# A two-layer recurrent and attention net on one core: sums, gating and output projection between the layers rearranged over GpSimd, TensorE, VectorE and ScalarE

## The reference, cut to what matters

```
xn = layernorm(x)
# layer 0: a gated pair of recurrences, and 8 experts (top 2, capacity 640 rows each)
for t in range(256):                       # for each of the 16 sequences
    h_ssm = silu(h_ssm @ A.T + bx[t]);  y_ssm = h_ssm @ Cw.T + Cb + dx[t]
    h_rnn = GRU(h_rnn, ih[t]);          y_rnn = h_rnn @ proj_w.T + proj_b
    s[t]  = g0[t] * y_ssm + g1[t] * y_rnn
moe = w0 * expert[top0](xn) + w1 * expert[top1](xn)     # silu(moe) below
x   = x + s * silu(moe)
# layer 1: attention with 16 heads of 64, and 160 experts (top 8)
xn = layernorm(x)
x  = x + attention(xn) * silu(ffn160(xn))
```

## Time and profile before

| what | value |
|---|---|
| time before, median of 3 runs | 2086.22 us (2082.82 to 2088.34) |
| time of the profiled execution | 2083.28 us |
| its span in the profile | 2081.5 us |
| its mean granted TensorE clock | 0.938 |
| busy: PE, DVE, ACT, POOL | 1823.4, 1272.7, 888.1, 625.7 us |

### The profile page before, as it was taken

The page is one execution under the profiler, slowest core; times in us unless marked ns, Lnnn a source line. Parts: engine busy times, 40 slices in busy tenths (PEclk is TensorE's granted clock), DMA queues, the critical chain, the costliest instruction groups (busy, mean ns, idle before and its releaser), DMA issues.

```text
span 2081.5 us, 49942 instructions
## 1 busy us (share of the span) xinstructions
PE 1823.4 (88%) x14389; PEld 1623.3 (78%) x14390; DVE 1272.7 (61%) x4624; ACT 888.1 (43%) x2899; POOL 625.7 (30%) x661
## 2 busy tenths in 40 slices
PE   4699999999999999369999999688888988888786
PEld 2467999999997777239999998677777788787785
DVE  4444444544554434888888888344444677777776
ACT  2212444444442211316666665344444555555453
POOL 0074000000006400016677773000000555555551
PEclk9799999999999975669999999899999999999997
DMA  9511011111001100301111112444444211111111
GB/s 377 238 47 37 23 36 35 36 44 40 25 26 47 30 0 0 159 9 48 48 49 52 51 50 101 147 141 149 149 145 141 58 40 39 38 40 40 38 40 54
DMA packets 153497, 149.29 MB, mean 72 GB/s; under 512 B 16931, under 2 KB 134374, under 8 KB 153062
## 3 DMA queue, kind: packets, MB, share of 16 engines
q1 hardware_dynamic: 130820, 100.98, 14.6%
q0 software_dynamic: 21760, 46.18, 7.5%
q10 hardware_dynamic: 866, 1.51, 0.2%
HBM read 70.95 MB, written 77.66 MB: 71 GB/s over the span
## 4 chain that ended last, share of the span: by engine, by line
PE 67%; DMA 11%; DVE 10%; issue 8%; ACT 2%; POOL 1%; DVEq 1%; ACTq 0%; POOLq 0%; SPq 0%
DMA rows_g<-ys_dram,slot 10%; PE ps_y L735 8%; PE ps_t L940 5%; PE ps_up L1042 5%; PE ps_y L793 4%; PE ps_up L784 4%; PE ps_t L1053 4%; PE ps_up L916 4%; PE ps_y L929 3%; PE ps_t L753 3%; PE ps_t L751 3%; PE ps_rec L750 3%; PE ps_rec L748 3%; PE ps_rec L884 2%; PE ps_rec L1020 2%
## 5 line engine op out<-in xcount | busy, mean ns | idle before, releaser
L479 POOL DMA_INDIRECT rows_g<-ys_dram,slot x256 | 242.7, 948 | 529.8 <-DMA ys_dram<-slots_y 346.7
L623 ACT ACTIVATE probs<-ps_up,negmax 128x256 f32<-128x256 f32 x512 | 240.5, 483 | 323.9 <-DVE negmax L1447 323.9
L469 POOL DMA_INDIRECT xs_dram<-xn_tok,slot x256 | 249.4, 974 | 314.6 <-DVE slot L1349 215.1
L940 PE MATMUL ps_t<-v_sb,probsT 128*128 128x64 f32 x2048 | 261.2, 271 | 2.1 <-DVE ctx_sb L1430 1.5
L940 PEld LDWEIGHTS ps_t<-v_sb,probsT 128*128 128x128 f32 x2048 | 252.7, 194 | 4.3 <-issue 4.2
L735 PE MATMUL ps_y<-zeros 128*128 128x512 bf16 x752 | 219.8, 382 | 0.0
L1206 DVE SCALAR_TENSOR_TENSOR mixn<-ps_rec,cols_sb,th_r 128x16 f32<-128x16 f32 x256 | 59.8, 234 | 245.1 <-PE ps_rec L750 143.1
L1447 DVE TENSOR_REDUCE negmax<-ps_up 128x2 f32<-128x512 f32 x256 | 164.7, 685 | 31.2 <-PE ps_up L916 30.9
L916 PE MATMUL ps_up<-kT,qT 64*128 64x256 f32 x1536 | 127.7, 299 | 60.6 <-DVE kT L1403 60.0
L916 PEld LDWEIGHTS ps_up<-kT,qT 64*128 64x128 f32 x1536 | 101.7, 190 | 81.2 <-issue 60.8
L929 PE MATMUL ps_y<-misc,probs 128*128 128x128 f32 x1024 | 163.7, 283 | 0.6 <-ACT probs L623 0.5
(11 more groups left out here) (241 smaller groups left out, 4386.0 us busy)
## 6 DMA issues: line engine op xcount, KB each, us to landing
xs_dram<-zeros SPq DMA_DIRECT2D x52, 512.0 KB, 9.3
slots_x<-xs_dram SPq DMA_DIRECT2D x88, 256.0 KB, 3.0
ys_dram<-slots_y SPq DMA_DIRECT2D x84, 256.0 KB, 2.5
slots_x<-xs_dram SPq DMA_DIRECT2D x41, 128.0 KB, 2.1
ys_dram<-slots_y SPq DMA_DIRECT2D x40, 128.0 KB, 1.8
gate<-w_gate SPq DMA_DIRECT2D x1, 5120.0 KB, 20.7
down<-w_down SPq DMA_DIRECT2D x1, 5120.0 KB, 15.2
w_sb<-w POOLq DMA_DIRECT2D x16, 256.0 KB, 4.8
```

What stands on the lines that cost most here:

```text
L469: nc.gpsimd.indirect_dma_start(xs_dram, bass.IndirectOffsetOnAxis(ap=slot[:, n, k:k + 1], axis=0), xn_tok[:, n, :], None).then_inc(scatter ...
L479: nc.gpsimd.indirect_dma_start(rows_g[:, i % 16, :], None, ys_dram, bass.IndirectOffsetOnAxis(ap=slot[:, i // TOPK1, i % TOPK1:i % TOPK1 + ...
L623: nc.scalar.activation(probs[:, a, i, :], ps_s[a][:, T * i:T * i + T], ACT.Exp, bias=negmax[:, a, i:i + 1], accum_out=sums[:, j % 4, i, a: ...
L940: last = nc.tensor.matmul(ps_ctx[:, P * i + HD * a:P * i + HD * a + HD], probsT[:, a, kc, P * i:P * i + P], v_sb[:, j % 2, kc, HD * a:HD * ...
```

## The change

Five edits, all between the layers or for them:

1. `hist_s`'s bias row is written by GpSimd at the start of the kernel (64 partitions in place of 32), and the recurrent step writes only the 64 partitions of the state. The memset after the recurrence is gone.
2. The sum of the expert rows goes to GpSimd: per tile two products with a weight per token and one sum, 128 columns each, issued one tile behind the two gathers (`sum_rows`).
3. The output projection runs in groups of four tiles, each kind of result in one bank of 512 columns. TensorE waits once in four tiles, ScalarE takes the tanh of a quarter behind each of the first four groups, and VectorE makes silu behind each even group.
4. The product with s and the sum with x go to GpSimd, in pieces of 512 columns (`sil_ready`, `gated`, `x1_ready`). Mean and subtraction of layer norm 2 begin behind the odd groups from the fourth; the squares go to another buffer. The casts of the weights come before the product with the reciprocal, and ScalarE's scaling of the query weights, and an empty sigmoid, before the copies of the turned tokens. The weight loads wait for `var_ready` too.
5. In the placement loop, the offset comes in by one more matmul of one row (line 919 of the changed kernel), and VectorE's add is gone: it multiplies by the mask straight from PSUM, which is also `place_read`.

```diff
@@ GpSimd
+            nc.gpsimd.memset(hist_s[64:128, :, :], 2.0).then_inc(bias_rows, 1)
+            def sum_rows(n):
+                nc.gpsimd.tensor_scalar(xn_tok[:, n, :], xn_tok[:, n, :], w0[:, n, 0:1], None, ALU.mult) \
+                    .then_inc(row_scaled, 1)
+                nc.gpsimd.tensor_scalar(second[:, n, :], second[:, n, :], w0[:, n, 1:2], None, ALU.mult) \
+                    .then_inc(row_scaled, 1)
+                pool.wait_ge(row_scaled, 2 * n + 2)
+                nc.gpsimd.tensor_tensor(xn_tok[:, n, :], xn_tok[:, n, :], second[:, n, :], ALU.add) \
+                    .then_inc(acc_final, 1)
...
+                if n:
+                    sum_rows(n - 1)
...
+            for g in range(NG):
+                tok = slice(512 * g, 512 * g + 512)
+                pool.wait_ge(sil_ready, g // 2 + 1)
+                pool.wait_ge(y_used, g + 1)
+                nc.gpsimd.tensor_tensor(sil[:, tok], sil[:, tok], s_all[:, tok], ALU.mult).then_inc(gated, 1)
+                pool.wait_ge(gated, g + 1)
+                nc.gpsimd.tensor_tensor(x_all[:, tok], x_all[:, tok], sil[:, tok], ALU.add).then_inc(x1_ready, 1)
@@ SyncE
             sp.wait_ge(x1_ready, NG)
+            sp.wait_ge(var_ready, 2)
@@ ScalarE
-            for n in range(NT):
-                act.wait_ge(y_ready, n + 1)
-                nc.scalar.mul(gin[:, 1, n // 2, 128 * (n % 2):128 * (n % 2) + 128], ps_up[n % 2][:, 0:128],
-                              gate[:, n, 0:1]).then_inc(y_scaled, 1)
+            for g in range(NG):
+                act.wait_ge(y_ready, g + 1)
...
+                if g < 4:
+                    act.wait_ge(acc_final, 8 * g + 8)
...
+                if g == 5:
+                    square(1, squares, 0)
+            for c in range(1, 4):
+                square(1, squares, c)
+            deviation(1)
+            act.wait_ge(attn_loaded, 16 * 10)
@@ TensorE, output projection
-            pe.wait_ge(bias_rows, 1)
-            for n in range(NT):
-                b, h = n // 2, n % 2
-                if n >= 2:
-                    pe.wait_ge(y_scaled, n - 1)
-                    pe.wait_ge(y_used, n - 1)
...
+            for g in range(NG):
+                if g >= 2:
+                    pe.wait_ge(y_scaled, 4 * (g - 1))
+                    pe.wait_ge(y_used, g - 1)
+                for n in range(4 * g, 4 * g + 4):
...
+                last.then_inc(y_ready, 1)
@@ TensorE, placement
+            pe.wait_ge(offs_ready, 1)
             pe.wait_ge(probs1_ready, NT)
...
+                nc.tensor.matmul(dst, ones[0:1, :], offs[0:1, :], start=True, stop=False)
                 if n:
                     nc.tensor.matmul(dst, upper_b[0:NT, n - 1:n].to_broadcast([NT, P]), tile_tot,
-                                     start=True, stop=False)
-                nc.tensor.matmul(dst, upper_b, chosen[:, n, :], start=(n == 0), stop=True).then_inc(place_mm, 1)
+                                     start=False, stop=False)
+                nc.tensor.matmul(dst, upper_b, chosen[:, n, :], start=False, stop=True).then_inc(place_mm, 1)
@@ VectorE
-            V.memset(hist_s[64:96, :, :], 2.0).then_inc(bias_rows, 1)
...
+                if g % 2 == 0:
+                    q = slice(512 * g, 512 * g + 1024)
+                    dve.wait_ge(silu_th, g // 2 + 1)
...
+                elif g >= 3:
+                    dve.wait_ge(sil_ready, g // 2)
+                    dve.wait_ge(x1_ready, g - 1)
+                    centre(1, g // 2 - 1)
...
+            centre(1, 3)
+            variance(1, squares)
...
+            scale_rows(1)
...
             for n in range(NT):
                 dve.wait_ge(place_mm, n + 1)
-                V.tensor_tensor(place[:, n, :], ps_rec[n % 2][:, 0:E1], offs, ALU.add).then_inc(place_read, 1)
+                V.tensor_tensor(place[:, n, :], ps_rec[n % 2][:, 0:E1], chosen[:, n, :], ALU.mult) \
+                    .then_inc(place_read, 1)
                 if n >= 1:
-                    placed(n - 1)
-                if n >= 2:
-                    places_of(n - 2)
+                    places_of(n - 1)
```

More of the change, by code:

```diff
@@ L121, in build @@
         newn = sb("newn", [P, 16])
+        sil = gin[:, 0, :, :].rearrange("p b t -> p (b t)")
+        s_all = gin[:, 2, :, :].rearrange("p b t -> p (b t)")
+        squares = gin[:, 3, :, :].rearrange("p b t -> p (b t)")
+        x_all = x_tok[:, :, :].rearrange("p n d -> p (n d)")
         scr = hist_g[:, :, :].rearrange("p b t -> p (b t)")
@@ L248, in build @@
         zeroed0 = sem("zeroed0")
-        first_scaled = sem("first_scaled")
+        row_scaled = sem("row_scaled")
+        sil_ready = sem("sil_ready")
+        gated = sem("gated")
         scattered0 = [sem("scattered0_even"), sem("scattered0_odd")]
@@ L461, in _ @@
                         .then_inc(gathered0[k], 16)
+                if n:
+                    sum_rows(n - 1)
+            for k in range(2):
+                pool.wait_ge(gathered0[k], 16 * NT)
+            sum_rows(NT - 1)
+            for g in range(NG):
[5 more added lines that the diff above has]
+                nc.gpsimd.tensor_tensor(x_all[:, tok], x_all[:, tok], sil[:, tok], ALU.add).then_inc(x1_ready, 1)
             pool.wait_ge(slots_ready, 1)
@@ L492, in _, with square, deviation @@
             act.dma_start(b1_sb[:, :], b1).then_inc(consts_loaded, 16)
[L494 to L499, removed]
+            def square(layer, scratch, c):
+                act.wait_ge(centred, 4 * layer + c + 1)
+                nc.scalar.activation(scratch[:, 1024 * c:1024 * c + 1024],
+                                     xn_tok[:, 8 * c:8 * c + 8, :].rearrange("p n d -> p (n d)"),
+                                     ACT.Square).then_inc(squared, 1)
+            def deviation(layer):
                 act.wait_ge(var_ready, layer + 1)
@@ L502, in layer_norm @@
                     .then_inc(std_ready, 1)
-            layer_norm(0, scr2)
+            for c in range(4):
+                square(0, scr2, c)
+            deviation(0)
             for g in range(NG):
@@ L1092, in _, with centre, variance @@
             chain(V.memset(eps_col[:, :], EPS))
[L1094 to L1102, removed]
-                        .then_inc(centred, 1)
+            def centre(layer, c):
+                s = slice(8 * c, 8 * c + 8)
+                chain(V.tensor_reduce(ln_sum[:, s], x_tok[:, s, :], AX_X, ALU.add))
+                chain(V.tensor_scalar(ln_mean[:, s], ln_sum[:, s], 1.0 / P, None, ALU.mult))
+                V.tensor_tensor(xn_tok[:, s, :], x_tok[:, s, :], across(ln_mean[:, s], [P, 8, P]), ALU.subtract) \
+                    .then_inc(centred, 1)
+            def variance(layer, scratch):
                 for c in range(4):
@@ L1110, in layer_norm, with scale_rows @@
                 red.then_inc(var_ready, 1)
+            def scale_rows(layer):
                 dve.wait_ge(std_ready, layer + 1)
@@ L1116, in layer_norm @@
                         .then_inc(xn_ready, 1)
-            layer_norm(0, scr2)
+            for c in range(4):
+                dve.wait_ge(x_loaded[c], 16)
+                centre(0, c)
+            variance(0, scr2)
+            scale_rows(0)
             dve.wait_ge(consts_loaded, 16 * 7)
```

98 lines of the change are left out of this document (39 added, 59 removed).

## The result

The changed kernel takes 2063.99 us (median of 4 runs, 2056.23 to 2066.88) where the kernel before takes 2087.28 (median of 4, 2082.82 to 2092.88): 23.3 us less, a ratio of 0.988 with a 95% interval of 0.9845 to 0.9918. Forecast were 2055 and a range of 2037 to 2076. The profiled execution is the fastest of the four, 2056.23 with a span of 2054.4, against a span of 2081.5 before: 27.0 less.

A forecast was written before the change was run, and what follows sets the result against it. TensorE was taken to bound the kernel (67% of the chain), its projection at half clock. Terms −4.4, −35.2, −4.5, −3.3, +16.7 and +0.5 sum to −30.2: 2053.1 us for the profiled execution, 2055 as median, range 2037 to 2076.

The forecast's parts named there:

- The clock in the projection: Output projection: without idle time TensorE enters and stays at clock 1.00, 1.2 us per tile instead of 2.30: −35.2 us.
- The rival in which the clock falls during the projection: Output projection: clock 0.50 comes back within it, the −35.2 is lost, total 2088 to 2090 us; chance 0.12.
- a busy stretch keeps its clock: Reason given for the projection staying at full clock: a window at 873 to 893 us, clock 0.91, 16.49 of 20 busy.
- The start: Start of the projection: without the memset TensorE goes on at about 753.0 instead of 757.44, −4.4 us.
- GpSimd beside the recurrence: Recurrence: GpSimd's expert-row sums overlap 112 us of it and cause a few short collisions, +0.5 us, bounds 0 and 33.
- GpSimd's products: Expert-row sums beside the recurrence: each GpSimd product of 128 columns takes 0.30 us; the sums are covered.
- its pieces of 512 columns: Gating behind the projection groups: each GpSimd instruction of 512 columns takes 1.2 us.
- The slow-GpSimd rival: Expert-row sums and gating: GpSimd delays the first transpose; no change at 0.75 us per 128 columns, 2115 at 0.944; chance 0.05.
- To the first transpose: Projection's end to first transpose: 29.1 us instead of 33.65, with loads and casts standing alone, −4.5 us, bounds −9 to +1.
- To the placement loop: Router, first transpose to placement: −2.3 us from an earlier first sigmoid and −1.0 from no clock dip, −3.3 together.
- Placement loop: Placement loop: a third, one-row matmul makes TensorE the pace at 1.25 us per tile, +16.7 us, bounds +3 to +28.
- cheap placement: Rival, placement loop: the one-row matmul costs little, VectorE keeps the pace, +3 instead of +16.7, total 2041 us; chance 0.13.

The follow-up runs named there:

- e2: Kernel before with only the bias row's memset moved to GpSimd and the state update narrowed to 64 partitions: 2053.28 us, ratio 0.9823.
- e3: Changed kernel with VectorE's memset put back between recurrence and projection, TensorE waiting for it: 2100.17 us in one run.
- e4: Changed kernel without GpSimd's products and sum of the expert rows, gathers kept: 2064.37 us in one run; last 64 recurrent steps 157.97 us.
- e8: Changed kernel with the old placement loop, early weight loads with later casts, and gating on VectorE: 2029.62 us, ratio 0.9729.
- e10: Changed kernel with two unread full matmuls added per placement-loop tile: loop 35.4 us; total 2482.19 us, unusable because transfers stood still.
- e9: Changed kernel with weight loads issued when the last tiles are combined and casts behind the product with the reciprocal: 2047.08 us, ratio 0.9798.
- e7: Changed kernel with the gating product and sum on VectorE instead of GpSimd, in the same pieces: 2060.40 us in one run.
- e1: Changed kernel with the placement loop of before (VectorE adds the offset, no one-row matmul): 2047.71 us, ratio 0.9801.
- e6: Changed kernel with one unread full matmul added per placement-loop tile: 2075.81 us in one run, loop 49.5 us.

## Why the prediction was right

- *The clock in the projection* carried it. The cause of the low clock, the idle time, was right (e2, e3), and so was the size: −32.7 for −35.2. The term was mis-sized by the tile, 1.28 us for 1.2, so 41.0 for 38.4 in all; halving the times at 0.50 would give 1.15, and that bound wasn't reached. The rival in which the clock falls during the projection did not come, in any of the nine kernels without an idle time ahead of it. Its reason for the clock to stay is not sound, though: "a busy stretch keeps its clock" rested on a window whose mean of 0.91 is itself a dip (0.50 for 3.4 us), and the placement loop, busy throughout, lost the clock at 863. That it stayed in the projection is measured; why it stays there and not in the loop is not shown, so that step was in part luck. The prediction also worked with groups of four alone; e2 shows that the grouping adds nothing.
- *The start:* −4.4 for the idle time came as worked out (from the last state of the recurrence to the first projection matmul 4.9 us before, 0.5 after), but was given back: the sum of the stage is +0.1. The mis-sized term is GpSimd beside the recurrence, +0.5 in the forecast and +2.6 by e4, within a bound of 33 that was far too wide. Another +1.8 stands ahead of the recurrence (its first state at 118.48, 116.65 before). Five more kernels with the sums had 118.9 to 119.7, but e8 and e10, which have them too, had 116.8 and 116.5, and e2 and e4 116.9 and 116.7. What decides it stays open; as it comes and goes among kernels that share the edits, they alone are not the cause.
- *GpSimd's products* were mis-sized by a factor of two (0.61 for 0.30), its pieces of 512 columns were not (1.27 for 1.2), except that three of the 16 started beside VectorE's subtraction and took 2.33; the very last is one of them. The estimate of 1.12 from the figure for 2048 columns in the Trainium skill, GPSIMD Engine Reference, section 3 "Performance versus the Vector engine", came out 12% under the measured 1.27, and the measured decides. The slow-GpSimd rival had its break-even at 0.75 for 128 columns and was nearer than I thought; the sums end 1.3 us before the projection begins.
- *To the first transpose:* −3.7 for −4.5. Each of its steps is in the rows: issue of the loads 12.75 us behind the projection's end (11.6; the held last piece on GpSimd is 1.1 of it), wait 12.62 (12.5). What the prediction took as given, loads issued behind the sums of squares with the casts alone behind them, is where e9 finds 15.2 us.
- *To the placement loop:* −2.6 for −3.3. The first sigmoid comes 7.13 us after the first transpose, as worked out (7.3). The part that the clock has in it varies: e3 and e7, with the same edits in this stage, had 0.50 for 6.8 us of it and took 35.25 and 35.23 us, hardly less than the 35.7 of before.
- *Placement loop:* +14.8 for +16.7, 1.21 us per tile for 1.25 (32 times 1.25 is 40.0, where the prediction wrote 39.1); cheap placement, the rival, did not come. The low clock was taken as given ("it is cold already"), but the loop starts at 1.00, and its first tiles take 0.71 each. At that pace all 32 would take about 23 us, an estimate from these two tiles, against 22.4 before: nearly all of the +14.8 is the third matmul at the low clock, not the third matmul as such.
- *The end.* −2.9 was not forecast. The last stage alone is 4.8 us shorter, and nothing ties that to the change: kernels that share its edits came out both ways. Behind the last gather of expert rows the kernels need about 31.7, 36.7 or 39.7 us, and in the ten profiled traces other than the disturbed one the length goes with the granted clock of the last matmuls: 31.7 or 31.8 at 1.00 (changed kernel, e1, e3, e7, e8), 36.6 to 39.7 at 0.50 (before, e2, e4, e6, e9). Which of these an execution gets may be a good part of the spread of 10 us between runs of the changed kernel; only profiled executions show the stage, so that is not shown.

What is left of the 23.3 us, then, by the medians: one edit that is worth 38, and four that together cost 15. Sizes in the traces: +14.8 the placement loop and +2.6 the sums beside the recurrence, against −3.7 and −2.6 between projection and placement; the rest lies in the pieces that vary from run to run.

## What to carry to other kernels

When TensorE is busy throughout a stretch, look at its granted clock and at what came ahead of the stretch; here 4.2 us of idle time, made by one memset, cost 33 us behind it. Look also whether the clock comes back in the stretch: in the transposes it did, in the projection it did not. Moving one operation from the engine that sets the pace to another is worth only what that engine has free at its clock of the moment; the one-row matmul turned a loop of 0.70 us per tile into one of 1.21. And a load that was hidden has to be checked again when the order around it changes: its wait condition may keep it back until nothing is left to hide it.

## What the runs showed of the hardware that I had not expected

- TensorE's granted clock fell from 1.00 to 0.50 in the middle of a stretch of 100% busy time (863 us), where matmuls over 1, 32 and 128 rows of 160 columns alternate, and stayed at 1.00 in the same loop with two unread matmuls of 128 rows and 480 columns added (35.4 us with them, 37.2 without, 49.5 with one).
- A stretch that starts at 0.50 behind an idle time can come back or not: the transposes, from 828.45 on, were at 1.00 again from 832.2, and the projection of before stayed at 0.50 for all of its 73.6 us, busy throughout.
- The projection took 40.96 us in nine kernels and 73.64 in the two with the idle time; nothing lay between.
- GpSimd's product with a weight per token (128 columns, 0.61 to 0.63 us) is slower than its sum of two tensors of the same size (0.46 us).
- VectorE's `omz`, a product and sum with constants and one input, was held up to 598 ns beside GpSimd's arithmetic, 393 without it, though it has only one input in SBUF. The runs don't separate why.
